# Probabilities times values in alternating column halves of TensorE, and layer 3's late steps without the 384-column products

## The chip, the cores and the metric

The kernel runs on one core of a Trainium2 chip. The metric is device time in microseconds (us) of one execution. The before kernel was timed in three runs; a fourth execution was profiled.

## What is computed

A small vision tower on 32 images of 84x84: patches of 16x16 give 25 tokens an image (800 in all) of 192 channels. Four layers follow, each `h = layernorm(h + f(h))`: linear attention, a top-2 mixture of eight experts, differential attention with 12 heads, and attention with low-rank adapters picked by a gate. The change touches the two attention layers at the end (layers 2 and 3, counted from 0). Cut to what matters:

```python
# layer 2: two score sets, out1 - exp(lambda) * out2
out1 = softmax(q[0] @ k[0].T / sqrt(D)) @ v
out2 = softmax(q[1] @ k[1].T / sqrt(D)) @ v
h = layernorm(h + (out1 - lam * out2) @ Wo + bo)
# layer 3: one score set; qkv = x @ Wqkv.T + bqkv + 2 * gated low-rank delta
attn = softmax(q @ k.T * SCALE)
h = layernorm(h + (attn @ v) @ Wproj.T + bproj)
```

Attention is within an image, so each softmax is over 25 tokens.

## The kernel before, in words

Each engine has its program written out by hand, and semaphores tie the programs together. An engine takes its instructions in the order of the code: a wait holds all that stands behind it.

In layers 2 and 3 the 32 images are taken in eight groups of four (`G = 8`, `IG = 4`, 100 tokens a group). `call` is 0 in layer 2 and 1 in layer 3. A group g passes these stages:

- `scores(call, g)` (TensorE, L956): query times key, 32-column outputs in PSUM;
- the shift (VectorE, L1797 and L1798, two pieces in layer 3): row maximum and subtraction;
- `exp_out` (ScalarE, L1343);
- the norm (VectorE): in layer 3 L1807 (sum), L1808 (reciprocal), L1815 and L1818 (products with the reciprocal), which leave the probabilities p of the group. In layer 2 GpSimd adds the two sets (L640, L641);
- `turn` (TensorE, L966): three transposes of p, copied to SBUF by ScalarE (`p1T_out`, L1164);
- `times_v` (TensorE, L980): twelve products of a 128x64 block of values, the weights, with 25 columns of turned probabilities. The three head stacks b = 0, 1, 2 write PSUM partitions 0 to 63, 64 to 127 and again 0 to 63, so they use column half 0, 64 and 0 of the array. All write PSUM bank 5; ScalarE copies it out as `oa` and `ob` (`o_out`), and the next `times_v` waits for that (`o1_done`);
- `project` (TensorE, L991 and L992): the output projection of a tile of 128 tokens, when its groups are there. Tiles 0, 1, 2 come in steps 5, 6, 7, tile 3 in step 9, the others in step 10.

VectorE's order in both layers is shift(0), shift(1), norm(0), shift(2), norm(1), and so on: norm(g-1) stands behind shift(g).

`late_steps` writes TensorE's steps 4 to 10: in step s come `keep_busy`, `scores(s)`, `turn(s-2)`, `times_v(s-3)` and the projection, if there is one. `keep_busy(bank, 1, 384)` (L680) is one product of the identity with 384 columns of a weight; nothing reads its result. It stands in steps 4 to 9.

GpSimd fills `v_bd`, the block of values, in `place_values` (L631). Its second half in layer 3 is needed by `times_v(4)`.

A float32 product shows in the trace as two MATMUL records and two LDWEIGHTS records (PE and PEld): a `times_v` is 24 of each.

Of the kernel before, what the change touches and what calls it, by code (L numbers as in the profile page):

```python
# [27 lines left out]
N = NB * NB  # L28
# [8 lines left out]
IG = 4  # L37
G = B // IG
# [51 lines left out]
def build(nc, io):  # L90
    with ExitStack() as ctx:
        def sb(name, shape, dt=F32, scope=ctx):
            return scope.enter_context(nc.sbuf_tensor(name, shape, dt))
# [4 lines left out]
        ps = ctx.enter_context(nc.psum_tensor("ps", [128, 8, 512], F32))  # L98
# [73 lines left out]
        v_bd = sb("v_bd", [128, B, 3, 64], scope=late)  # L172
# [69 lines left out]
        p1T = sb("p1T", [128, 2, 3, 128])  # L242
# [426 lines left out]
        def last_group(t):  # L669

            return (128 * t + rows(t) - 1) // GT
# [3 lines left out]
        def _(pe):  # L675
            def keep_busy(bank, n, width=128):


                for _ in range(n):
                    pe.matmul(ps[:, bank, 0:width], ident, w1a[:, 0:width] if width > 128 else ident, start=True, stop=True)  # L680
# [24 lines left out]
            for k in range(KCH):  # L705
# [11 lines left out]
                for n in range(2):  # L717
# [3 lines left out]
                    mm = pe.matmul(ps[:, 2 + n, 0:HALF], hi[:, CA:WC], lo[:, tok], start=False, stop=final)  # L721
# [140 lines left out]
            for t in range(TT - 1):  # L862
                pe.matmul(ps[:, RANK_BANK, E * (t + 1):E * (TT + 1)].rearrange("p (t e) -> p t e", e=E), every, view(pick_mask[:, t, :], [[0, TT - t], [1, E]]),
                          start=(t == 0), stop=False, skip_group_check=True)
# [6 lines left out]
            for i in range(PICKS):  # L871
# [3 lines left out]
                mm = pe.matmul(ps[:, IDS_BANK, 0:3 * NBLK], in_row[0:n, i, :], blk_ids[0:n, i, :, :].rearrange("p b v -> p (b v)"), start=(i == 0), stop=(i == PICKS - 1))  # L875
# [64 lines left out]
            def values(call, n, terms, k):  # L940

                for g in range(4 * n, 4 * n + 4):
                    out = ps[:, V_BANKS[call][n][(g % 4) // 2], 256 * (g % 2):256 * (g % 2) + C]
                    x, w = terms[k]
                    mm = pe.matmul(out, padded(x, g), w, start=(k == 0 and g % 2 == 0), stop=(k == len(terms) - 1), skip_group_check=True)  # L945
                return mm

            def scores(call, g, slots):
                if g >= 2:
                    pe.wait_ge(s1_shifted, G * call + g - 1)  # L950
                for bank, slot, row, stack in slots:
                    for i in range(IG):
                        tok = GT * g + N * i
                        keys = k_bd[row:row + 64, stack, :, tok:tok + N]
                        at = tok - HALF * (g // 4)
                        mm = pe.matmul(ps[32 * i:32 * i + 32, 2 * (g % 2) + bank, 4 * N * slot:4 * N * slot + 4 * N],  # L956
                                       qT[row:row + 64, stack, g // 4, at:at + 32], keys, start=True, stop=True)
                mm.then_inc(s1_ready, 1)

            def turn(call, g):  # L960
                n = G * call + g
                pe.wait_ge(p1_ready, n + 1)
                if g >= 1:
                    pe.wait_ge(p1T_done, n)
                for b in range(3):
                    mm = pe.transpose(ps[:, 4, 128 * b:128 * b + 128], p1[:, g % 2, b, :, :], ident[:, :])  # L966
                mm.then_inc(p1T_ready, 1)

            def times_v(call, g):
                n = G * call + g  # L970
                pe.wait_ge(p1T_done, n + 1)
                if g % 4 == 0:
                    pe.wait_ge(v_placed, 32 * call + 16 * (g // 4) + 16)
                if g >= 1:
                    pe.wait_ge(o1_done, n)
                for b in range(3):
                    for i in range(IG):
                        rr = 64 * (b % 2)
                        at = (128 if b == 2 else 0) + N * i
                        mm = pe.matmul(ps[rr:rr + 64, 5, at:at + N], v_bd[:, IG * g + i, b, :],  # L980
                                       p1T[:, g % 2, b, 32 * i:32 * i + N], start=True, stop=True)
                mm.then_inc(o1_ready, 1)

            def project(call, t, wa, wb):
                pe.wait_ge(o1_done, G * call + last_group(t) + 1)
                if t >= 4 and t % 2 == 0:

                    pe.wait_ge(summed, PAIRS * (1 + call) + t // 2 - 1)
                cols = slice(128 * t, 128 * t + rows(t))
                out = ps[0:rows(t), PROJ_BANKS[t // 2], (t % 2) * C:(t % 2) * C + C]  # L990
                pe.matmul(out, oa[:, cols], wa, start=True, stop=False)  # L991
                pe.matmul(out, ob[:, cols], wb, start=False, stop=True).then_inc(proj_ready, 1)  # L992

            def late_steps(call, slots, wa, wb):


                for step in range(4, G + 3):
                    if step < G + 2:
                        keep_busy(2 * (step % 2), 1, 384)
                    if step < G:  # L1000
                        if step == 4:
                            pe.wait_ge(qk_act, [10, 14][call])
                        scores(call, step, slots)
                    if step <= G + 1:
                        turn(call, step - 2)
                    times_v(call, step - 3)
                    for t in range(TT):
                        if last_group(t) + 4 == step:
                            project(call, t, wa, wb)
                for t in range(TT):  # L1010
                    if last_group(t) + 4 > G + 2:
                        project(call, t, wa, wb)
# [56 lines left out]
            scores(0, 3, slots1)  # L1069
            turn(0, 1)  # L1070
            times_v(0, 0)
            late_steps(0, slots1, wo1a, wo1b)


# [53 lines left out]
            for k in range(3):  # L1128
                mm = values(1, 0, second_v, k)
# [21 lines left out]
            scores(1, 3, slots2)  # L1151
            turn(1, 1)
            times_v(1, 0)
            pe.wait_ge(qk_act, 15)
            for k in range(3):
                mm = values(1, 1, second_v, k)
            mm.then_inc(v_ready, 1)
            late_steps(1, slots2, wp2a, wp2b)


# [804 lines left out]
```

## Time and profile before

| | |
|---|---|
| time, median of 3 runs | 297.06 us (296.89 to 299.38) |
| the profiled execution: time | 298.84 us |
| its span, first to last instruction | 297.0 us |
| outside the span | 1.84 us |
| PE (TensorE) busy | 268.6 us, 90% |
| DVE (VectorE) busy | 161.7 us, 54% |
| ACT (ScalarE) busy | 122.1 us, 41% |
| POOL (GpSimd) busy | 119.9 us, 40% |
| mean granted TensorE clock | 0.983 |

Busy time counts a matmul from its start to its modelled end, so PE can be busy and yet wait inside. The chain of waits says what sets the end; the timeline says when each piece runs.

### The profile page before, as it was taken

How to read it: one execution, taken by the hardware profiler on the slowest of the kernel's cores; microseconds unless marked ns; L12 is line 12 of the kernel's file. 1: busy time of each engine (PE TensorE's matmuls, PEld its weight loads, DVE VectorE, ACT ScalarE, POOL GpSimd, SP SyncE). 2: the span in 40 equal slices, each digit the busy share in tenths (PEclk: the TensorE clock that was granted, in tenths of full speed). 3: DMA queues.
4: the chain of work that ended last, by engine and by line, in shares of the span. 5: the costliest groups of instructions: out<-in, count | busy, mean ns of one | idle time of the engine just before them, and what ended most of it. 6: DMA issues, size and time to landing. Idle time of an engine off the chain costs nothing.

```text
span 297.0 us, 6621 instructions
## 1 busy us (share of the span) xinstructions
PE 268.6 (90%) x2575; PEld 222.7 (75%) x2575; DVE 161.7 (54%) x486; ACT 122.1 (41%) x350; POOL 119.9 (40%) x189
## 2 busy tenths in 40 slices
PE   8989998978999999999999689976979799999990
PEld 8968688536999999999996368854758657577780
DVE  4786886883332321233200858578796383656765
ACT  5667875422234442324440046763321214644220
POOL 8661211316555567664323148145432100436011
PEclk9988999988999999999999999999999999999997
DMA  7999950252489999994003300000000000000002
GB/s 230 386 423 420 253 227 2 79 177 79 158 319 351 317 344 335 349 297 170 29 26 95 100 0 2 0 2 2 2 4 2 0 1 2 0 2 2 2 1 82
DMA packets 10113, 39.15 MB, mean 132 GB/s; under 512 B 1594, under 2 KB 5434, under 8 KB 7291
## 3 DMA queue, kind: packets, MB, share of 16 engines
q1 hardware_dynamic: 8163, 34.81, 32.6%
q0 software_dynamic: 1920, 3.93, 4.8%
q8 instruction: 20, 0.33, 0.5%
q14 instruction: 10, 0.08, 0.1%
HBM read 35.54 MB, written 3.19 MB: 130 GB/s over the span
## 4 chain that ended last, share of the span: by engine, by line
PE 69%; DVE 15%; issue 6%; ACT 4%; POOL 3%; DMA 3%; SPq 0%; POOLq 0%; DVEq 0%; ACTq 0%
PE ps L919 13%; PE ps L897 10%; PE ps L907 5%; PE ps L945 5%; PE ps L980 4%; PE ps L680 3%; PE ps L1094 3%; PE ps L956 2%; PE ps L966 2%; PE ps L991 2%; PE ps L704 2%; PE ps L804 1%; DVE st L1797 1%; DVE s L1798 1%; PE ps L992 1%
## 5 line engine op out<-in xcount | busy, mean ns | idle before, releaser
L680 PE MATMUL ps<-w1a,consts 128*128 128x384 f32 x96 | 36.6, 514 | 1.3 <-DVE h_tok L1588 1.3
L631 POOL COPY v_bd<-v_f 32x192 f32<-32x192 f32 x64 | 22.4, 351 | 34.3 <-ACT v_f L1164 30.5
L1293 ACT ACTIVATE hid<-ps,w1t 128x128 f32<-128x128 f32 x72 | 19.9, 375 | 34.9 <-PE ps L908 31.3
L577 POOL DMA_INDIRECT y_rows<-ys,to_row x20 | 19.8, 988 | 25.6 <-DVE ys L1749 23.2
L547 POOL TENSOR_TENSOR rstd<-veps,neg_half 128x2 f32<-128x2 f32 (+1 forms) x16 | 10.7, 669 | 45.4 <-DVE veps L1606 45.3
L571 POOL DMA_INDIRECT xs<-x_rows,from_row x20 | 19.6, 981 | 22.1 <-PE ps L885 11.1
L1736 DVE COPY xga<-ps 128x128 f32<-128x128 f32 x20 | 5.8, 292 | 40.2 <-PE ps L885 39.9
L680 PEld LDWEIGHTS ps<-w1a,consts 128*128 128x128 f32 x96 | 17.7, 195 | 11.0 <-DVE h_tok L1588 1.9
L919 PE MATMUL ps<-w1t,hid 128*128 128x192 f32 x144 | 24.6, 326 | 0.0
L919 PEld LDWEIGHTS ps<-w1t,hid 128*128 128x128 f32 x144 | 23.3, 190 | 0.0
L1797 DVE TENSOR_REDUCE st<-ps 128x24 f32<-128x600 f32 (+2 forms) x24 | 11.2, 467 | 20.4 <-PE ps L956 20.3
L1343 ACT ACTIVATE e<-s 128x600 f32<-128x600 f32 (+1 forms) x16 | 9.3, 580 | 27.1 <-DVE s L1798 27.1
L980 PEld LDWEIGHTS ps<-p1T,v_bd 128*64 128x64 f32 x384 | 17.0, 137 | 3.0 <-issue 3.0
L897 PE MATMUL ps<-xga,w1t 128*128 128x128 f32 x144 | 18.7, 280 | 0.5 <-DVE xga L1736 0.5
L980 PE MATMUL ps<-p1T,v_bd 128*64 128x25 f32 x384 | 18.6, 220 | 0.1
L897 PEld LDWEIGHTS ps<-xga,w1t 128*128 128x128 f32 x144 | 17.2, 191 | 1.4 <-issue 0.7
L1335 ACT ACTIVATE k_bd<-ps,consts 128x400 f32<-128x400 f32 (+1 forms) x28 | 14.3, 595 | 0.5 <-PE ps L1038 0.4
L956 PEld LDWEIGHTS ps<-k_bd,qT 64*32 64x32 f32 x576 | 7.6, 105 | 8.8 <-issue 6.9
L640 POOL TENSOR_TENSOR p<-e 128x200 f32<-128x200 f32 x8 | 4.9, 608 | 20.9 <-DVE e L1812 17.2
L966 PE MATMUL ps<-consts,p 128*128 128x128 f32 x48 | 8.5, 287 | 5.1 <-POOL p L641 4.8
L956 PE MATMUL ps<-k_bd,qT 64*32 64x100 f32 x576 | 11.2, 252 | 1.5 <-ACT qT L1164 1.0
L1164 ACT ACTIVATE xpa<-ps 128x500 f32<-128x500 f32 (+3 forms) x6 | 1.8, 356 | 24.5 <-PE ps L695 24.5
(300 smaller groups left out, 670.3 us busy)
## 6 DMA issues: line engine op xcount, KB each, us to landing
w1t<-in_wt SPq DMA_DIRECT2D x12, 1256.0 KB, 9.6
w1t_mid<-in_wt SPq DMA_DIRECT2D x3, 1256.0 KB, 11.0
w1t_top<-in_wt SPq DMA_DIRECT2D x3, 1256.0 KB, 10.8
pat<-in_pat SPq DMA_DIRECT2D x6, 496.0 KB, 6.3
w1t_low<-in_wt SPq DMA_DIRECT2D x2, 1256.0 KB, 7.3
w1a<-in_w1a SPq DMA_DIRECT2D x1, 1322.0 KB
y<-y_rows SPq DMA_DIRECT2D x6, 192.0 KB, 3.2
w1b<-in_w1b SPq DMA_DIRECT2D x1, 835.2 KB
```

The source lines that it names most:

```text
L571: pool.indirect_dma_start(xs[:, b, :], None, io["x_rows"], bass.IndirectOffsetOnAxis(from_row[:, j:j + 1], 0)).then_inc(gathered[b], 16)
L577: pool.indirect_dma_start(io["y_rows"], bass.IndirectOffsetOnAxis(to_row[:, j:j + 1], 0), ys[:, b, :], None).then_inc(scattered[b], 16)
L631: pool.tensor_copy(dst, src).then_inc(v_placed, 1)
L680: pe.matmul(ps[:, bank, 0:width], ident, w1a[:, 0:width] if width > 128 else ident, start=True, stop=True)
L897: mm = pe.matmul(hidden_out(j, k), w[:, 128 * k:128 * k + 128], xga[:, j % 2, :], start=(opens and k % HALF_HC == 0), stop=not opens, skip ...
L907: pe.matmul(hidden_out(j, k), w[0:CB, tail], xgb[0:CB, j % 2, :], start=(opens and k == 0), stop=not opens, skip_group_check=True)
L919: mm = pe.matmul(ps[:, Y_BANK[j % 2], 0:C], hid[:, j % 2, 128 * k:128 * k + 128], w[:, OUT_AT + C * k:OUT_AT + C * k + C], start=(k == 0), ...
L945: mm = pe.matmul(out, padded(x, g), w, start=(k == 0 and g % 2 == 0), stop=(k == len(terms) - 1), skip_group_check=True)
L956: mm = pe.matmul(ps[32 * i:32 * i + 32, 2 * (g % 2) + bank, 4 * N * slot:4 * N * slot + 4 * N], qT[row:row + 64, stack, g // 4, at:at + 32 ...
L966: mm = pe.transpose(ps[:, 4, 128 * b:128 * b + 128], p1[:, g % 2, b, :, :], ident[:, :])
L980: mm = pe.matmul(ps[rr:rr + 64, 5, at:at + N], v_bd[:, IG * g + i, b, :], p1T[:, g % 2, b, 32 * i:32 * i + N], start=True, stop=True)
L1293: ins = act.activation(hid[:, j % 2, 128 * k:128 * k + 128], hidden_out(j, k), ACT.Relu, bias=weights(j)[:, B1_AT + k:B1_AT + k + 1])
```

## The change

Two edits in TensorE's program. In `times_v` the loops over b and i change places: the twelve products are the same, and they now use the column halves in the order 0, 64, 0, 0, 64, 0, ... In `late_steps` the product that nothing reads stays in layer 2 and goes in layer 3, where there were six of them.

```diff
-                for b in range(3):
-                    for i in range(IG):
-                        rr = 64 * (b % 2)
-                        at = (128 if b == 2 else 0) + N * i
-                        mm = pe.matmul(ps[rr:rr + 64, 5, at:at + N], v_bd[:, IG * g + i, b, :],
-                                       p1T[:, g % 2, b, 32 * i:32 * i + N], start=True, stop=True)
+                for b, i in ((0, 0), (1, 0), (2, 0), (0, 1), (1, 1), (2, 1), (0, 2), (1, 2), (2, 2), (0, 3), (1, 3), (2, 3)):
+                    rr = 64 * (b % 2)
+                    at = (128 if b == 2 else 0) + N * i
+                    mm = pe.matmul(ps[rr:rr + 64, 5, at:at + N], v_bd[:, IG * g + i, b, :],
+                                   p1T[:, g % 2, b, 32 * i:32 * i + N], start=True, stop=True)
                 mm.then_inc(o1_ready, 1)
...
                 for step in range(4, G + 3):
-                    if step < G + 2:
+                    if call == 0 and step < G + 2:
                         keep_busy(2 * (step % 2), 1, 384)
```

TensorE's program in steps 4 and 5 of layer 3, before: an L680 product stands ahead of each block of scores (L956).

```order
L945 MATMUL ps<-w1a,hwT 128x192 x4
L680 MATMUL ps<-w1a,consts 128x384
L956 MATMUL ps<-k_bd,qT 32x100 [waits s1_shifted,qk_act]
L956 MATMUL ps<-k_bd,qT 32x100 x11
L966 MATMUL ps<-consts,p 128x128 [waits p1T_done,p1_ready]
L966 MATMUL ps<-consts,p 128x128 x2
L980 MATMUL ps<-p1T,v_bd 64x25 [waits o1_done,p1T_done]
L980 MATMUL ps<-p1T,v_bd 64x25 x11
L680 MATMUL ps<-w1a,consts 128x384
L956 MATMUL ps<-k_bd,qT 32x100 [waits s1_shifted]
```

The same place now; `times_v` is at L979 in the changed file.

```order
L945 MATMUL ps<-w1a,hwT 128x192 x4
L956 MATMUL ps<-k_bd,qT 32x100 [waits s1_shifted,qk_act]
L956 MATMUL ps<-k_bd,qT 32x100 x11
L966 MATMUL ps<-consts,p 128x128 [waits p1T_done,p1_ready]
L966 MATMUL ps<-consts,p 128x128 x2
L979 MATMUL ps<-p1T,v_bd 64x25 [waits o1_done,p1T_done]
L979 MATMUL ps<-p1T,v_bd 64x25 x11
L956 MATMUL ps<-k_bd,qT 32x100 [waits s1_shifted]
```

The scores follow the values or the projection directly. The twelve products of `times_v` read alike in both, since the rows do not show which column half one uses.

TensorE's program in steps 8 and 9 of layer 3, before: two L680 products ahead of the last two turns (L966).

```order
L992 MATMUL ps<-w1b,ob 128x192
L680 MATMUL ps<-w1a,consts 128x384
L966 MATMUL ps<-consts,p 128x128 [waits p1T_done,p1_ready]
L966 MATMUL ps<-consts,p 128x128 x2
L980 MATMUL ps<-p1T,v_bd 64x25 [waits o1_done,p1T_done]
L980 MATMUL ps<-p1T,v_bd 64x25 x11
L680 MATMUL ps<-w1a,consts 128x384
L966 MATMUL ps<-consts,p 128x128 [waits p1T_done,p1_ready]
```

And now:

```order
L991 MATMUL ps<-w1b,ob 128x192
L966 MATMUL ps<-consts,p 128x128 [waits p1T_done,p1_ready]
L966 MATMUL ps<-consts,p 128x128 x2
L979 MATMUL ps<-p1T,v_bd 64x25 [waits o1_done,p1T_done]
L979 MATMUL ps<-p1T,v_bd 64x25 x11
L966 MATMUL ps<-consts,p 128x128 [waits p1T_done,p1_ready]
```

The turn of a group stands right behind the work before it, and waits there for the group's probabilities (`p1_ready`). No other engine's program changes.

## Rows read from the trace of the kernel before

**Rows 1.** The page: busy time, share of the span, instructions

```profile
PE 268.6 (90%) x2575; PEld 222.7 (75%) x2575; DVE 161.7 (54%) x486; ACT 122.1 (41%) x350; POOL 119.9 (40%) x189
```

**Rows 2.** The chain that ended last: start us, us, what

```profile
221.06 1.10 PE ps L980 x24
...
267.90 0.65 PE ps L680 x2
...
270.60 0.84 PE ps L680 x2
```

**Rows 3.** Timeline of TensorE, layer 3, steps 4 to 6: start us, us, what

```profile
268.47 0.55 PE L956 MATMUL ps<-k_bd,qT 64*32 64x100 f32 x24
...
271.86 0.31 PEld L966 LDWEIGHTS ps<-consts,p 128*128 128x128 f32 x3 [0.17 <-DVE p L1818]
271.87 0.55 PE L966 MATMUL ps<-consts,p 128*128 128x128 f32 x3
...
273.44 0.59 PE L991 MATMUL ps<-w1a,oa 128*128 128x192 f32 x2
...
274.94 0.55 PE L956 MATMUL ps<-k_bd,qT 64*32 64x100 f32 x24
```

**Rows 4.** Timeline of VectorE and GpSimd, layer 3, steps 4 to 6

```profile
268.93 6.42 POOL L631 COPY v_bd<-v_f 32x192 f32<-32x192 f32 x16 [6.41 <-ACT v_f L1164]
...
269.09 0.37 DVE L1797 TENSOR_REDUCE st<-ps 128x8 f32<-128x200 f32 x1 [4.53 <-PE ps L956]
...
270.24 0.46 DVE L1807 TENSOR_REDUCE st<-e 128x12 f32<-128x300 f32 x1
...
271.41 0.40 DVE L1818 TENSOR_TENSOR p<-e,st 128x100 f32<-128x100 f32 x1
...
276.70 0.46 DVE L1807 TENSOR_REDUCE st<-e 128x12 f32<-128x300 f32 x1
...
277.74 0.26 DVE L1818 TENSOR_TENSOR p<-e,st 128x100 f32<-128x100 f32 x1
```

**Rows 5.** Timeline of TensorE and ScalarE, layer 3, steps 7 to 10

```profile
278.49 0.55 PE L956 MATMUL ps<-k_bd,qT 64*32 64x100 f32 x24
...
281.94 0.49 PE L966 MATMUL ps<-consts,p 128*128 128x128 f32 x3
...
282.36 1.17 PE L980 MATMUL ps<-p1T,v_bd 128*64 128x25 f32 x24
...
283.71 0.23 ACT L1164 ACTIVATE ob<-ps 64x100 f32<-64x100 f32 x1
...
284.63 1.17 PE L980 MATMUL ps<-p1T,v_bd 128*64 128x25 f32 x24
```

**Rows 6.** Timeline of TensorE's weight loads inside one `times_v` (L980), in narrow windows

```profile
272.34 1.06 PEld L980 LDWEIGHTS ps<-p1T,v_bd 128*64 128x64 f32 x24 [0.17 <-issue]
...
272.34 0.37 PEld L980 LDWEIGHTS ps<-p1T,v_bd 128*64 128x64 f32 x5 [0.17 <-issue]
...
272.61 0.25 PEld L980 LDWEIGHTS ps<-p1T,v_bd 128*64 128x64 f32 x5
...
273.15 0.25 PEld L980 LDWEIGHTS ps<-p1T,v_bd 128*64 128x64 f32 x3
```

**Rows 7.** `times_v` (L980), all its records: duration ns min/median/max, first and last start us

```profile
L980 PEld LDWEIGHTS ps<-p1T,v_bd x384: 132/138/138, 199.1 to 287.5; 128*64 128x64 f32 x192
L980 PE MATMUL ps<-p1T,v_bd x384: 208/217/238, 199.1 to 287.5; 128*64 128x25 f32 x192
```

**Rows 8.** Windows: stretch, length us, busy us (records) of PE, PEld, DVE, ACT, POOL, clock

```profile
17.30:20.70 3.40, 2.02 (x10) 1.03 (x8) 3.37 (x6) 2.24 (x5) 3.17 (x4) 1.00 1.00 417
20.70:24.10 3.40, 3.40 (x10) 2.93 (x11) 2.98 (x9) 2.32 (x7) 2.11 (x2) 0.50 1.03 424
...
218.70:222.10 3.40, 2.58 (x33) 1.77 (x31) 3.26 (x7) 0.54 (x2) 1.49 (x3) 1.00 0.00 0
...
228.90:232.30 3.40, 2.11 (x18) 1.73 (x17) 3.08 (x13) 1.20 (x4) 1.24 (x2) 1.00 0.00 0
```

## The prediction

> **What bounds the kernel now.** The page comes first: TensorE is busy 90% of the span, more than any other engine [rows 1]. Busy is not bound, so the chain that ended last comes next. It runs through TensorE for most of the two last layers. All six L680 products of layer 3 lie on it: four cost 0.65 us and two, those that follow a `times_v` directly, 0.84 us; one of each kind is shown [rows 2]. That is 4 x 0.65 + 2 x 0.84 = 4.28 us of chain. Of the sixteen `times_v` twelve are on it, 1.10 us each, of which one stands there: four in layer 2, eight in layer 3 [rows 2]. Third, the timeline of layer 3's steps shows what stands ready to take over. The reader is to look at where VectorE finishes a group's probabilities and where TensorE turns them.
>
> **Part one, the six products.** They go from the chain, so the first estimate is 4.28 us. It is an upper end, because VectorE and ScalarE have to keep up. I follow the steps one by one; "earlier" is against the trace of before.
>
> Step 4. The scores started at 268.47 [rows 3]; without 0.65 us ahead of them they start at 267.82. The shift begins 0.62 us behind the scores (269.09 after 268.47 [rows 3, 4]).
>
> Step 5. TensorE alone would come 0.65 + 0.84 = 1.49 us earlier to turn(3), and 0.06 us more by part two: 271.87 - 1.55 = 270.32. But p of group 3 isn't there. VectorE does shift(4), 1.15 us (269.09 to 270.24), then norm(3), 1.57 us (270.24 to 271.41 + 0.40 = 271.81) [rows 4]. Already in the trace of before turn(3) waits for L1818, and starts 0.05 us after its end [rows 3, 4]. Both move with scores(4), by 0.65 us. So turn(3) starts at 271.87 - 0.65 = 271.22 and TensorE stands still for 0.9 us: the step's own product brings nothing. The norm can't be quicker there. GpSimd's copies run from 268.93 to 275.35, and they start when `v_f` is written, ahead of all the products. Beside them the norm takes 1.57 us, after them 1.30 us (276.70 to 277.74 + 0.26 = 278.00) [rows 4]. That the copies are what slows it is my reading; no row here takes them away.
>
> Step 6. Shift(5) and norm(4) follow on VectorE without a gap, 271.2 + 1.15 + 1.52 = 273.87 (1.52 us lies between the two norms, nearer to the slow one, since the copies still run). TensorE: projection at 273.44 - 0.65 - 0.06 = 272.73, scores(6) at 274.94 [rows 3] - 0.65 - 0.06 - 0.65 = 273.58, turn(4) 0.5 us later at 274.06, just behind the p of 273.87. Gain so far 1.36 us.
>
> Step 7. From here shift and norm take 2.45 us and TensorE's step, 3.55 us before (278.49 - 274.94 [rows 3, 5]), takes 3.55 - 0.65 - 0.06 = 2.84. TensorE leads again: scores(7) at 276.42, gain 2.07 us. Group 4's values need GpSimd's copies, done at 275.35, and come at 277.4: covered by 2 us.
>
> Step 8. There are no scores here, so TensorE would reach turn(6) at 276.42 + (281.94 - 278.49) - 0.65 - 0.06 = 279.16 [rows 5]. Its p is there at 276.42 + 0.62 + 1.15 + 1.30 = 279.49, and the turn starts at 279.55. Gain 2.39 us: 0.4 us of the product is lost to VectorE.
>
> Step 9. By TensorE's order `times_v(6)` would come another 0.84 + 0.06 us earlier, at 284.63 - 2.39 - 0.90 = 281.34. It waits for the copy of `ob` of the group before. That ended at 283.71 + 0.23 = 283.94, 1.58 us after its `times_v` started at 282.36 [rows 5]. With `times_v(5)` at 279.97 and 0.06 us shorter it ends at 281.49, so `times_v(6)` starts at 281.56, 3.07 us earlier.
>
> Behind that nothing new is late: the last two `times_v` bring 0.06 us each, and projections, VectorE's last layer norm and the last output follow TensorE as before. Layer 3 from step 4 on comes to 3.19 us, of which 0.28 us are part two's: the products alone bring 2.9 of their 4.28 us. Of the missing 1.4 us some 0.9 go to VectorE in step 5, 0.4 to VectorE in step 8, 0.1 or 0.2 to ScalarE's copy in step 9.
>
> **Part two, the column halves.** What overlaps now can be read from the starts of the weight loads, each 0.138 us long [rows 7]. At the start of a `times_v`, where all loads go to half 0, five span 0.37 us: (0.37 - 0.138) / 4 = 58 ns apart. Near its end, half 0 again, three span 0.25 us: 56 ns. In the middle, where b = 0 gives way to b = 1, five span 0.25 us: 28 ns apart [rows 6]. So within one half a load and its product follow each other, and across halves they run side by side, but only near the two places where the half changes. All 24 span 1.06 us, (1.06 - 0.138) / 23 = 40 ns on average.
>
> In the new order half 0 carries b = 0 and b = 2, 16 of the 24 records, and half 64 always has its 8 beside them. The floor is half 0's own chain: 15 intervals of 58 ns = 0.87 us, and 0.02 us for a first product that is longer (238 against 217 ns [rows 7]), 0.89 us. Before, the 24 starts take 0.92 us by the loads (1.06 - 0.138), and 0.95 us by the products (the block is 1.17 us [rows 5], less 0.22 for the last product [rows 7]). The gain is 0.03 to 0.06 us a call; I take 0.056, one interval of half 0, for that is what the hand-over from b = 0 to b = 2 leaves open. The bounds lie wide apart: were nothing overlapped any more, 23 x 58 = 1.33 us, a loss of 0.4 us a call; were all overlapped as in the middle, 23 x 28 = 0.64 us, a gain of 0.28 us, which half 0's 16 records exclude. I take the value next to the rows of half 0. On the chain: 4 in layer 2 and 6 in layer 3 that no wait swallows (those of steps 5 and 8 go into VectorE's waits), about 10 x 0.056 = 0.56 us, 0.28 of it counted above, so 0.28 us more.
>
> The trace shows loads of one half beside products of the other, though both use all 128 rows of the array [rows 6]. The Trainium skill (TensorE: Matmul & The Clock Gate, What overlaps and what doesn't) says that a weight load overlaps matmuls in flight only when its row group differs. By that rule the new order would bring nothing. The 28 ns above disagree.
>
> **The sum.** 3.19 + 0.28 = 3.47 us. The profiled execution took 298.84 us for a span of 297.0, so 1.84 us lie outside it, and it is 1.8 us above the median of 297.06. By its own time the changed kernel would be 298.84 - 3.5 = 295.3 us. All that changes is inside the span, so I take the same gain off the median: 297.06 - 3.5 = **293.6 us**, 1.2% faster. A difference of 1%, 3.0 us, is about what a measurement of this kernel can tell from none.
>
> **Rivals.**
>
> *The order of the halves brings nothing* (the engine looks ahead as far as it needs already, or the row-group rule holds): minus 0.56 us, 294.1. For it: the gain rests on a single interval a call. Against it: the middle rows, and half 0's gap between b = 0 and b = 2. Chance 0.12.
>
> *The clock falls in layer 3.* The products may hold it up. Clock before: it was half after 17.3 to 20.7, where TensorE was busy 2.02 of 3.40 us, and stayed full after 228.9 to 232.3 with 2.11, and 218.7 to 222.1 with 2.58 [rows 8]. Without the products layer 3's thinnest stretch is step 5 (0.9 us idle) and the three spare steps 8 to 10, busy at least 2.5 of 3.4 us. That speaks against a fall, but the margin to 2.02 is small and busy time isn't work. One stretch of 3.4 us at 1.2 GHz does half of its work: 1.7 us lost, 295.3 us. Chance 0.15. The Trainium skill (TensorE: Matmul & The Clock Gate, What's actually happening) says that "the default state is throttled, and activity releases the throttle"; the stretch at 0.50 that follows the thin one agrees with it.
>
> *Slower: changing halves costs instead of paying.* If each change of half makes the engine finish the product in flight, the overlap is gone: loads at 58 ns throughout, 1.33 instead of 0.92 us a call, 0.41 us x 12 on the chain = 4.9 us, against 2.9 us from the products: 299.1 us. It decides from a mean of about 50 ns between loads on: 2.9 / 12 = 0.24 us a call, over 23 intervals 10 ns above today's 40. Against it: the two changes of half in today's order cost nothing visible, they are where the spacing is 28 ns. Chance 0.06.
>
> *More is won*: VectorE's norm(3) is quicker than in the trace because it meets fewer copies, or ScalarE's copy in step 9 is no wait. Up to 4.28 + 12 x 0.056 = 4.95 us, 292.1. Chance 0.07.
>
> The rest, 0.60, is the forecast, with its own range of 292.9 to 294.6.
>
> **How the numbers follow.** Range: below it reaches to the full gain of 4.95 us, 292.1; above it takes in one stretch at half clock and the scatter of the runs, to 296.5. Outside are two stretches of low clock, the slower rival and a run like the 299.38. Faster by over 1% means under 294.1: three quarters or more of the forecast (0.48), half of the first rival's 0.12, and the 0.07: about 0.60. Slower by over 1%: 0.05. Within: 0.35.
>
> **What would show it.** In the changed profile: no L680 record among layer 3's steps. Turn(3) waits for L1818 with some 0.9 us of idle TensorE, and turn(6) with 0.4; `times_v(6)` waits for `ob`. Steps 6 to 7 are 2.84 us apart from scores to scores instead of 3.55. The 24 loads of a `times_v` span about 1.0 us instead of 1.06, and five of them anywhere but at the very end span 0.25. The clock row has no new dip ahead of the end. The forecast is wrong if the loads stand 58 ns apart, if a 0.50 shows within layer 3's steps, or if VectorE's waits sum to much over 1.3 us.

## The result and the profile after

Twenty executions of the changed kernel take 295.34 us (median), twenty of the kernel before 298.23 us. The ratio is 0.9896, with a 95% interval of 0.9874 to 0.9918: 1.0% faster, some 3.1 us. The profiled execution took 293.58 us, its span is 291.8 us. Executions more than 1.5% above the fastest of their kernel are left out of the ratio.

The page of the changed kernel, which answers to [rows 1]:

```profile
PE 261.7 (90%) x2563; PEld 217.4 (75%) x2563; DVE 161.6 (55%) x486; ACT 122.2 (42%) x350; POOL 120.0 (41%) x189
...
PEclk9999999979999999999999999999999999999997
```

The spans differ by 5.2 us, which is more than the change brings. TensorE starts the experts 1.7 us earlier after a half-clock stretch less, in code that the change doesn't touch (the first `times_v` starts at 197.3 us instead of 199.1). So I measure layer 3 from its last block of values, which starts at 266.43 us before and at 264.37 here:

```profile
264.37 1.47 PE L945 MATMUL ps<-w1a,hwT 128*128 128x192 f32 x8
```

From there to the end of the span it is 297.02 - 266.43 = 30.59 us before and 291.77 - 264.37 = 27.40 us now: 3.19 us less. From the first `times_v` to that block, most of layer 2 and the start of layer 3, it is 67.37 and 67.04 us: 0.33 us less.

Timeline of the changed kernel, steps 4 to 6 of layer 3, beside [rows 3, 4]. Line numbers are one lower behind L973:

```profile
265.77 0.55 PE L956 MATMUL ps<-k_bd,qT 64*32 64x100 f32 x24
...
266.38 0.37 DVE L1796 TENSOR_REDUCE st<-ps 128x8 f32<-128x200 f32 x1 [3.82 <-PE ps L956]
...
266.87 6.50 POOL L631 COPY v_bd<-v_f 32x192 f32<-32x192 f32 x16 [6.36 <-ACT v_f L1163]
...
267.53 0.46 DVE L1806 TENSOR_REDUCE st<-e 128x12 f32<-128x300 f32 x1
...
268.29 0.37 DVE L1814 TENSOR_TENSOR p<-e,st 128x200 f32<-128x200 f32 x1
268.57 0.40 DVE L1817 TENSOR_TENSOR p<-e,st 128x100 f32<-128x100 f32 x1
...
269.02 0.55 PE L966 MATMUL ps<-consts,p 128*128 128x128 f32 x3 [0.71 <-DVE p L1817]
...
271.39 0.55 PE L956 MATMUL ps<-k_bd,qT 64*32 64x100 f32 x24
```

Turn(3) now waits 0.71 us for L1817. VectorE had nothing to do for 3.82 us ahead of shift(4), yet norm(3) comes behind it. The same timeline for steps 7 to 9, beside [rows 5]:

```profile
274.24 0.55 PE L956 MATMUL ps<-k_bd,qT 64*32 64x100 f32 x24
...
277.36 0.55 PE L966 MATMUL ps<-consts,p 128*128 128x128 f32 x3 [0.20 <-DVE p L1817]
...
279.13 0.23 ACT L1163 ACTIVATE ob<-ps 64x100 f32<-64x100 f32 x1
...
279.51 1.08 PE L979 MATMUL ps<-p1T,v_bd 128*64 128x25 f32 x24
```

Turn(6) waits for L1817, and `times_v(6)` (279.51) starts right behind the copy of `ob` (279.13 + 0.23 = 279.36). A whole `times_v` and its first eight loads, beside [rows 6]:

```profile
269.50 1.01 PEld L979 LDWEIGHTS ps<-p1T,v_bd 128*64 128x64 f32 x24 [0.17 <-issue]
...
269.50 0.34 PEld L979 LDWEIGHTS ps<-p1T,v_bd 128*64 128x64 f32 x8 [0.17 <-issue]
```

The 24 loads span 1.01 us instead of 1.06, 38 ns apart on average. The first eight are (0.34 - 0.138) / 7 = 29 ns apart; the sixteen behind them, where half 0 has two products in a row again and again, take (1.01 - 0.34) / 16 = 42 ns each.

### The profile page after: what moved, and what is told of

It is laid out like the page before. It is cut to its first block, busy times and chain, and to the rows that moved or that the text cites. A ratio compares the mean times of both kernels' runs of the same rounds, so it can differ in the third digit from the quotient of the medians.

```text
span 291.8 us, 6597 instructions
## 1 busy us (share of the span) xinstructions
PE 261.7 (90%) x2563; PEld 217.4 (75%) x2563; DVE 161.6 (55%) x486; ACT 122.2 (42%) x350; POOL 120.0 (41%) x189
## 3 DMA queue, kind: packets, MB, share of 16 engines
HBM read 35.54 MB, written 3.19 MB: 133 GB/s over the span
## 4 chain that ended last, share of the span: by engine, by line
PE 68%; DVE 18%; issue 5%; ACT 4%; DMA 2%; POOL 1%; SPq 0%; POOLq 0%; DVEq 0%
PE ps L919 13%; PE ps L897 10%; PE ps L907 5%; PE ps L945 5%; PE ps L979 4%; PE ps L680 3%; PE ps L1093 3%; PE ps L956 2%; DVE st L1796 2%; DVE s L1797 2%; PE ps L966 2%; PE ps L804 2%; PE ps L990 1%; PE ps L704 1%; DVE stats L1598 1%
## 5 line engine op out<-in xcount | busy, mean ns | idle before, releaser
L680 PE MATMUL ps<-w1a,consts 128*128 128x384 f32 x84 | 31.6, 517 | 1.3 <-DVE h_tok L1587 1.3
L680 PEld LDWEIGHTS ps<-w1a,consts 128*128 128x128 f32 x84 | 16.0, 200 | 11.3 <-issue 2.2
L979 PEld LDWEIGHTS ps<-p1T,v_bd 128*64 128x64 f32 x384 | 16.1, 137 | 3.1 <-issue 3.1
L979 PE MATMUL ps<-p1T,v_bd 128*64 128x25 f32 x384 | 17.7, 221 | 0.2
L966 PE MATMUL ps<-consts,p 128*128 128x128 f32 x48 | 8.6, 289 | 6.1 <-POOL p L641 4.9
L956 PEld LDWEIGHTS ps<-k_bd,qT 64*32 64x32 f32 x576 | 7.6, 105 | 7.4 <-issue 5.4
L956 PE MATMUL ps<-k_bd,qT 64*32 64x100 f32 x576 | 11.2, 252 | 1.6 <-ACT qT L1163 1.1
L966 PEld LDWEIGHTS ps<-consts,p 128*128 128x128 f32 x48 | 5.0, 140 | 9.7 <-POOL p L641 5.2
```

## The experiments

Twelve kernels ran, each beside the kernel before on its chip. The granted clock explains much of the scatter, so this table compares executions of like clock (mean granted clock of the span). The mean clock sorts them and doesn't order them: the lowest times of both kernels lie at 0.987 to 0.989, and not at 0.995.

| kernel | at clock 0.994 to 0.996, us | at 0.987 to 0.992, lowest us |
|---|---|---|
| before | 297.3 to 297.8 (eight) | 296.97 |
| order of halves only (e1) | 296.91 to 297.06 (three) | 298.34 |
| products out only (e2) | 294.49, 294.69 | 294.38 |
| changed kernel (with e8) | 293.96 to 294.18 (five) | 293.33 |
| norm(3) ahead (e7) | 293.51 to 294.64 (four) | |
| norm(3) ahead, products in layer 2's waits (e10) | 294.25, 294.31 | 293.81 |
| norm(3) ahead, stack split (e9) | | 292.11 |
| e9 with four products more in layer 2 (e11) | | 292.36 |
| e9 with two products more in layer 2 (e12) | | 291.96 |

### Each part alone

e1 is the kernel before with the new order; e2 is the changed kernel with the old loops over b and i.

```diff
# e1
-                    if call == 0 and step < G + 2:
+                    if step < G + 2:
# e2
-                for b, i in ((0, 0), (1, 0), (2, 0), (0, 1), ...
+                for b in range(3):
+                    for i in range(IG):
```

> Only the new order of the column halves; layer 3 keeps its six 384-column products. Theory: each times_v is 0.05 to 0.06 us shorter (block 1.11 instead of 1.17 us, its 24 loads span 1.01 instead of 1.06), about ten of them on the chain, so 0.5 to 0.6 us less than before, ratio 0.998. The stretch from the last block of values in layer 3 (266.43 us before, 264.37 in the changed kernel) to the end of the span is 30.57 us before and 27.43 in the changed kernel: here about 30.25. Rival (the order does most of it): ratio 0.992 or less. Rival (the order costs): ratio over 1.00, loads 58 ns apart.

> Only the six 384-column products of layer 3 left out; times_v in the old order. Theory: 2.9 us less than before, ratio 0.990; the stretch from the last block of values to the end about 27.7 us; turn(3) waits some 0.7 us for L1818, turn(6) a little. Rival (the products hold the clock): a half-clock stretch among layer 3's steps and a gain of 1.2 us or less. Rival (all 4.28 us of the products are gained): ratio 0.986, stretch 26.3 us.

e1: ratio 1.0008 (0.9981 to 1.0035), which can't tell half a microsecond from nothing. At like clock it can be seen: 296.9 to 297.1 (three at 0.996) against 297.3 to 297.8 (eight at 0.994 or 0.995). Its trace has loads of 1.01 us, and 295.10 - 264.83 = 30.27 us from the last block of values on, 0.32 less than before. e2: ratio 0.9905 (0.9867 to 0.9944), 294.85 - 267.19 = 27.66 us, 2.93 less. The two sum to 3.25 in layer 3; both together gave 3.19. Neither rival of e2 came: no half-clock stretch lies among layer 3's steps, and turn(3) takes its part back:

```profile
271.84 0.55 PE L966 MATMUL ps<-consts,p 128*128 128x128 f32 x3 [0.65 <-DVE p L1818]
```

### What the halves cost, and when they overlap

e3 takes all products of half 0 first. e9 gives each half twelve of the 24 records, and has norm(3) ahead (below).

```diff
# e3
+                for b, i in ((0, 0), (0, 1), (0, 2), (0, 3), (2, 0), (2, 1), (2, 2), (2, 3), (1, 0), (1, 1), (1, 2), (1, 3)):
# e9
+                for b, i in ((0, 0), (1, 0), (0, 1), (1, 1), (0, 2), (1, 2), (0, 3), (1, 3), (2, 0), (2, 2), (2, 1), (2, 3)):
-                    rr = 64 * (b % 2)
+                    rr = 64 * (b % 2 if b < 2 else i // 2)
# ScalarE, o_out: ob in two copies
-                copy(ob[0:CB, GT * g:GT * g + GT], ps[0:CB, 5, 128:128 + GT]).then_inc(o1_done, 1)
+                copy(ob[0:CB, GT * g:GT * g + 2 * N], ps[0:CB, 5, 128:128 + 2 * N])
+                copy(ob[0:CB, GT * g + 2 * N:GT * g + GT], ps[CB:128, 5, 128 + 2 * N:128 + GT]).then_inc(o1_done, 1)
```

> As the changed kernel, but times_v does all eight products of half 0 (b = 0, then b = 2) and then the four of half 64 (b = 1). Theory (halves overlap only where the engine can look ahead to the other half): one hand-over instead of two, and the last products alone: half 0's 16 records at 58 ns, then half 64's 8 with some 3 of them overlapped, so the 24 loads span about 0.138 + 20 x 0.058 = 1.3 us instead of 1.01. Rival (the engine looks ahead over the whole call, so order doesn't matter): 1.0 us. Rival (nothing overlaps): 1.47 us.

> norm(3) ahead of shift(4), and in times_v the third head stack shared between the halves: images 0 and 1 of a group in half 0, images 2 and 3 in half 64, so each half carries 12 of the 24 records; ScalarE copies ob in two pieces. Theory (the busier half's own chain sets the length, 58 ns a record): 24 loads span 0.138 + 23 x 0.029 = 0.80 us instead of 1.01, a times_v is 0.2 us shorter, and the extra copy costs about 0.15 us where times_v waits for ob (layer 3, step 9); from the last block of values to the end 26.3 us against 26.96 with norm(3) ahead alone; at a clock of 0.995 about 293.0 us. Rival (another limit comes first, loads no closer than 38 ns): no shorter, and slower by the copies.

Weight loads of one `times_v` in e3, all and the first twelve:

```profile
273.93 1.27 PEld L979 LDWEIGHTS ps<-p1T,v_bd 128*64 128x64 f32 x24 [0.17 <-issue]
...
273.93 0.77 PEld L979 LDWEIGHTS ps<-p1T,v_bd 128*64 128x64 f32 x12 [0.17 <-issue]
```

And in e9:

```profile
271.52 0.78 PEld L979 LDWEIGHTS ps<-p1T,v_bd 128*64 128x64 f32 x24 [0.17 <-issue]
```

The expected 1.3 and 0.80 us are there. (e3's one execution, 299.29 us, had a half-clock stretch in layer 2, so only its layer 3, at full clock, is read.) (1.27 - 0.138) / 0.058 = 19.5 intervals of 58 ns, 3.5 fewer than the 23 of no overlap, and none of them are saved among the first twelve loads ((0.77 - 0.138) / 11 = 57 ns apart): only the hand-over to half 64 overlaps, three or four records of it. From the last block of values to the end e3 takes 28.69 us, 1.3 more than the changed kernel; that is 0.26 us for each of five calls, as many as the prediction counted for this stretch. (0.78 - 0.138) / 23 = 28 ns on average, the spacing that the middle rows of [rows 6] showed: both halves work all the time. So the same twelve products take 1.27, 1.06, 1.01 or 0.78 us by the order and the share of the halves alone. All weights use the 128 rows of the array, so the Trainium skill's sentence on row groups (TensorE: Matmul & The Clock Gate, What overlaps and what doesn't) doesn't hold for column halves here.

e9's stretch to the end is 290.34 - 264.21 = 26.13 us (26.3 expected), and from the first `times_v` to that block it takes 66.39 us against 67.04, so layer 2 gains as well. ScalarE's extra copy shows where it was expected, as `times_v(6)` waits for `ob`:

```profile
278.42 0.89 PE L979 MATMUL ps<-p1T,v_bd 128*64 128x25 f32 x24 [0.28 <-ACT ob L1163]
```

Its ratio is 0.989 (0.984 to 0.994) for all that, no better than the changed kernel's: two executions took 292.1 us at a clock of 0.992, but three took 294.7 to 296.0 at 0.962 to 0.964, and one 302.2 at 0.949.

### Who waits in layer 3

e4 leaves two of the six products standing. e5 leaves out GpSimd's second set of copies in layer 3, so groups 4 to 7 are multiplied with old values; `times_v` waits for the first set alone. e7 moves norm(3).

```diff
# e4
-                    if call == 0 and step < G + 2:
+                    if step < G + 2 and (call == 0 or step in (5, 8)):
# e5
-            place_values(1, 1, 0, 16)
-                    pe.wait_ge(v_placed, 32 * call + 16 * (g // 4) + 16)
+                    pe.wait_ge(v_placed, 48 if call else 16 * (g // 4) + 16)
# e7
+                    if call == 1 and step == 4:
+                        norm(3)
                     if step < G:
                         shift(step)
-                    if step >= 1:
+                    if step >= 1 and (call == 0 or step != 4):
                         norm(step - 1)
```

> As the changed kernel, but two of layer 3's six products stand again, in steps 5 and 8, where TensorE waits for VectorE. Theory: the one in step 5 costs nothing (turn(3) is held by L1818 either way), the one in step 8 costs about 0.3 us. From the last block of values to the end 27.7 us against 27.43. Rival (each product costs its 0.65 to 0.84 us): 28.9 us.

> As the changed kernel, but GpSimd leaves out the second set of sixteen copies into v_bd in layer 3, so groups 4 to 7 of layer 3 are multiplied with old values. Theory (GpSimd's copies slow VectorE's products L1814 and L1817 beside them): norm(3) takes 1.30 us instead of the 1.44 of the changed kernel, L1817 0.26 instead of 0.40; TensorE's wait at turn(3), 0.71 us in the changed kernel, falls by 0.15 us; stretch from the last block of values to the end 27.25 us instead of 27.4. Rival (the copies have nothing to do with it): norm and wait as in the changed kernel.

> As the changed kernel, but in layer 3 VectorE does norm(3) ahead of shift(4), while it waits for the scores of group 4. Theory (turn(3) waits only because norm(3) stands behind shift(4)): the 0.71 us wait at turn(3) goes, nothing else becomes late, and the stretch from the last block of values to the end is 26.7 instead of 27.4 us; ratio to before 0.987. Rival (the wait comes back at turn(4) or turn(5), for VectorE is full): stretch 27.2 us or more.

e4: 27.69 us from the last block of values to the end, against 27.40 (27.7 expected). Two products of 0.81 and 0.91 us of TensorE cost 0.3 us together. The one in step 5 is hidden: turn(3) starts at 270.84, 4.72 us behind the block of values, against 4.65 us in the changed kernel.

e5: the wait at turn(3) falls from 0.71 to 0.56 us and L1817's product (L1816 there) takes 0.26 instead of 0.40 us:

```profile
271.67 0.26 DVE L1816 TENSOR_TENSOR p<-e,st 128x100 f32<-128x100 f32 x1
...
271.98 0.55 PE L965 MATMUL ps<-consts,p 128*128 128x128 f32 x3 [0.56 <-DVE p L1816]
```

The stretch is 27.24 us (27.25 expected). So the copies do slow VectorE's product beside them. Only the last one, though: L1814 takes 0.37 us in the changed kernel with the copies and in e5 (L1813 there) without them.

e7: VectorE's wait is gone, but 0.44 us are gained, not 0.7: the stretch is 26.96 us instead of 27.40. The next one in line is ScalarE, whose copy of turn(2) stands behind exp(4), and so behind shift(4):

```profile
270.11 0.52 PE L966 MATMUL ps<-consts,p 128*128 128x128 f32 x3 [0.31 <-ACT p1T L1163]
```

Neither expectation was right: the wait neither went nor came back through VectorE. At a clock of 0.995 or 0.996 three of e7's executions take 293.5 to 293.7 us, 0.4 under the changed kernel; the profiled one, whose stretch was just read, takes 294.6. The ratio is 0.982 (0.978 to 0.987) from these four; two more took 299.8 and 303.3 us at 0.964 and 0.957.

### The clock

e6 leaves layer 2's six products out too. e8 is the changed kernel again. e10 to e12 put products where TensorE waits in layer 2: e10 on e7, the other two on e9.

```diff
# e6
-                    if call == 0 and step < G + 2:
-                        keep_busy(2 * (step % 2), 1, 384)
# e10 (g in (4, 6)), e11 (g in (3, 5, 6)), e12 (g == 3)
-                        keep_busy(2 * (step % 2), 1, 384)
+                        keep_busy(2 * (step % 2), 2 if step == 4 else 1, 384)
# turn, behind the wait for p1T_done and ahead of the one for p1_ready
+                if call == 0 and g in (4, 6):
+                    keep_busy(4, 1, 384)
```

> As the changed kernel, and layer 2's six 384-column products are left out too. Theory (layer 2's steps are set by VectorE and GpSimd): little is gained, 0.1 us at step 5 and 0.3 us at step 9, from the first times_v of layer 2 to the last block of values in layer 3 66.6 us instead of 67.04, if the clock stays; but layer 2's steps have thin stretches, so half-clock stretches there come more often and the median is not better than the changed kernel's. Rival (they cost like those of layer 3): 2 us less, ratio 0.983. Rival (the products hold the clock in layer 2): several half-clock stretches in layer 2, ratio 0.995 or more.

> The changed kernel again, for its clock. Theory (half-clock stretches come by the phase of the chip's own clock control, not by layer 3's missing products): runs at a mean granted clock of 0.994 to 0.996 take 294.0 us, 3.45 less than those of before at that clock, and a low one (0.971) comes from stretches in layer 2 or ahead of it. Rival: the profile shows a half-clock stretch among layer 3's steps.

> norm(3) ahead of shift(4), and in layer 2 three more 384-column products where TensorE waits: a second one in step 4, and one ahead of the wait of turn(4) and of turn(6). Theory (TensorE's thin stretches in layer 2 let the clock fall in some executions): their work is hidden, at a clock of 0.995 the time is 293.6 us as with norm(3) ahead alone, and no execution shows a clock of 0.96 to 0.98 from layer 2. Rival (the clock falls as often as before): about one in four at 0.97, 296.5 us. Rival (the products aren't hidden): 0.3 us or more over 293.6 at 0.995.

> norm(3) ahead, the third stack split over both halves, and in layer 2 four more 384-column products, now where TensorE waits longest: a second one in step 4, and one ahead of the waits of turn(3), turn(5) and turn(6) (1.08, 0.83 and 0.82 us of idle TensorE in the kernel before, against 0.65 to 0.84 us for a product). Theory (they are hidden there, and they hold the clock): 292.1 to 292.5 us at a clock of 0.987 to 0.995, no execution at 0.96 to 0.98, median under 293.3. Rival (not hidden): 292.9 us or more at 0.995. Rival (the clock falls anyway): executions at 0.96 with 294.7 us and more, as without them.

> As the run before, with two of the four products: the second one in step 4 and the one ahead of the wait of turn(3). Theory (the clock falls after layer 2's steps 4 and 5): as good as four products, median under 293.3 and no execution at 0.96. Rival (it also falls later): some executions at 0.96 to 0.98, 294.7 us or more.

e6 is slower than the kernel before, ratio 1.017 (1.012 to 1.022), and its four executions all have a clock of 0.92 to 0.94. The second rival of its expectation came, as one long stretch. Stretches of its trace (length, busy us of PE, PEld, DVE, ACT, POOL, granted clock):

```profile
196.80:200.20 3.40, 1.89 (x53) 1.46 (x41) 2.85 (x6) 1.65 (x6) 1.35 (x4) 0.99 0.00 0
200.20:237.70 37.50, 35.47 (x416) 28.61 (x417) 23.66 (x56) 8.15 (x25) 11.93 (x27) 0.50 0.01 2
```

After a stretch with 1.89 us of TensorE in 3.40 the clock is at 1.2 GHz for 37.5 us, through the rest of layer 2 and into layer 3, though busy time reads 95%. It costs 76.77 - 67.04 = 9.7 us from the first `times_v` to layer 3's last values.

e5 was caught in a lesser form of it. Up to layer 3 its TensorE program is the changed kernel's:

```profile
199.00:202.40 3.40, 1.76 (x59) 1.15 (x59) 2.61 (x6) 1.27 (x5) 1.59 (x4) 1.00 0.03 5
202.40:212.60 10.20, 10.20 (x131) 7.32 (x135) 5.92 (x11) 2.82 (x8) 5.38 (x15) 0.50 0.01 2
```

Those 10.2 us at half clock cost 3.2 us (70.21 against 67.04), and its mean clock is 0.971. Six of the changed kernel's 26 executions (e8 with them) have that clock and take 296.5 to 297.3 us; of the kernel before, 5 of the 56 whose clock is on record have 0.969 to 0.971 and take 300.4 to 302.2. With the deeper falls (0.947 to 0.957, 300.8 us and more) it is 10 of 26 and 13 of 56. e2's trace has two such stretches, 3.4 us each, in layer 2, where its program is the kernel's before. e3's and e11's traces have one each there too. So in the traces the stretches start in code that the removed products of layer 3 don't touch; no trace was kept of a low execution of the changed kernel itself. Whether the shorter `times_v` makes them more frequent in layer 2, these counts don't decide.

e8: two executions at 0.995 and 0.996 take 294.18 and 294.05 us, 3.4 us less than before at that clock, and no half-clock stretch lies in layer 3 in its trace.

e10: no execution below 0.983, 293.8 to 295.3 us. But at 0.995 it takes 294.3 us, 0.6 more than e7: I had put the product of turn(4) where TensorE waits 0.26 us, not where it waits longest. From the first `times_v` to layer 3's last values e10 takes 67.70 us, 0.67 more than e7. In e12, with the long waits chosen, two products cost 0.10 us there (66.49 against e9's 66.39). e11's four did not hold the clock: its trace has 3.4 us at half clock in layer 2 (67.22 us for the same way), so it can't say whether they are hidden, and its median misses the 293.3 expected. e11: ratio 0.985 (0.980 to 0.990), median 293.62 us, clock 0.973 to 0.992. e12: ratio 0.982 (0.978 to 0.987), median 292.77 us, 291.96 to 294.05, clock 0.973 to 0.992. Six executions are few, and the clock still sags to 0.973 in one of each; but e12's slowest is faster than the changed kernel's median. e12 is 1.8% under the kernel before. Against the changed kernel's 0.990 (0.987 to 0.992) the intervals only just part, and e7 without any of this has the same ratio, once its two low executions are left out; what e12 adds is that none of its six fell that far.

## Why the prediction was right, point by point

From the last block of values on, the six products went as the steps said:

| step | earlier by, forecast | measured |
|---|---|---|
| 4, scores(4) | 0.65 | 0.64 |
| 5, turn(3) | 0.65 | 0.79 |
| 6, scores(6) | 1.36 | 1.49 |
| 7, scores(7) | 2.07 | 2.19 |
| 8, turn(6) | 2.39 | 2.52 |
| 9, `times_v(6)` | 3.07 | 3.06 |
| end of the span | 3.19 | 3.19 |

The 0.13 us more from step 5 on are norm(3)'s: 1.44 us (267.53 to 268.97) instead of 1.57. The prediction said that the norm can't be quicker there, and that was wrong. GpSimd's copies start behind `v_f`, as said, and run beside the whole norm, but L1814 took 0.37 instead of 0.50 us: only the last multiplication was slowed. In norm(3) it takes 0.50 us in the kernel before and in e1, and 0.37 in the changed kernel, e2, e3, e4 and e8, where step 4's product is gone; why it escapes the copies then isn't shown. At `times_v(5)` 0.08 us of that are left, and the hand-over from `ob` to `times_v(6)`, 0.15 us instead of the 0.07 that I took, uses them up, so the end agrees. That the two cancel is luck. Idle TensorE ahead of turn(3) and turn(6) reads 0.71 and 0.20 us by the products, where 0.9 and 0.4 were forecast; 0.13 us of the first difference is norm(3)'s. The rest is in the counting: the profile counts from the modelled end of the product before, the forecast from the moment at which TensorE could have gone on. From scores(7) to turn(6) it is 3.12 us, with 3.13 forecast. The cause by VectorE is shown twice: e4 puts a product into step 5 for nothing, e5 shortens the wait by taking the copies away.

Part two was forecast at 0.056 us a call: the block fell from 1.17 to 1.11 us. Layer 2 and the start of layer 3 gained 0.33 us (0.28 forecast), and e1's 0.32 us in layer 3 answers to 0.28. One thing in it was off: five loads were to span 0.25 us anywhere but at the very end, and that holds for the first eight but not throughout; the average came out because half 0's sixteen records set the length, as said. The rule on row groups, one form of the first rival, fell with e9.

The sum, 3.47 us, is 3.19 + 0.33 = 3.52 by the traces, and 3.4 us at like clock. The measured median moved by 2.9 us and the ratio by 3.1, and the predicted 293.6 is 1.7 us under 295.34. Two things lie between. The median of three executions before, 297.06, lay low: twenty give 298.23, and that is 1.2 of the 1.7 us. The rest, some 0.6, is the forecast's 3.5 against the 2.9 between the medians, and there the clock has a part: a quarter of the changed kernel's executions fell to 0.971, more than of the kernel before, which may be chance. "Faster by over 1%" hangs on the edge: the interval of the ratio holds 0.99.

That is near the rival on the clock, and there the prediction had the place wrong. It priced one stretch of 3.4 us among layer 3's steps at 1.7 us. Layer 3's thinnest stretch, from 266.9 us on, has 2.69 of 3.40 us busy and kept its clock, and no trace has a half-clock stretch from layer 3's step 4 to TensorE's last product. Apart from single stretches ahead of the experts, as in [rows 8], the falls in the traces begin in layer 2 and last 3.4, 10.2 or 37.5 us. The kernel before falls too, by its mean clocks, but none of its low executions was profiled. In e5 10.2 us cost 3.2, a third of its length and not a half; VectorE and GpSimd set part of the steps there, which is a likely reason and not a tested one. The slower rival is refuted by e9: changes of half cost nothing.

## What to carry to other kernels

Ask of each product that only keeps an engine busy whether the engine waits there anyway: in layer 3, where TensorE led, six cost 2.9 us, while in layer 2, where it waits for VectorE and GpSimd, taking six out made the kernel slower, for the clock fell (ratio 1.017, against 0.989 for the changed kernel beside it). When work leaves the leading engine, walk the steps and look who stands next; here it was VectorE's program order, then ScalarE's. Small products in one column half can be sped up by giving the other half an equal share, in turn: 1.06 us became 0.78 for the same work.

## What the hardware showed that I had not expected

Full occupation by the profile doesn't say how long a fall lasts. At 1.2 GHz TensorE was busy 35.47 of 37.50 us in e6, and 10.20 of 10.20 us in e5, before the clock came back, while in the kernel before [rows 8] and in e11's layer 2 it came back after a single stretch with 3.40 of 3.40 us busy. What sets the length is open; no run here varied it alone. The order of the column halves also sets how much of their work overlaps: with eight products of one half in a row, only three or four records of the other half ran beside them (e3), and with the halves strictly in turn all of them did (e9).
